# Gathering ready-made key and value rows in the attention edge stage of a graph kernel

## The chip, the cores and the metric

One Trainium2 chip, one of its cores. The metric is the device time of one execution in microseconds (us), the median over several runs; lower is better.

## The reference

Four message-passing layers run over one graph of 50,000 nodes and 50,000 edges, the edges sorted by destination `dst`, 128 features throughout. The change touches the second layer, a sparse attention with 8 heads of 16 features. Its input is `h`, the node features behind a layer norm and a ReLU:

```python
K = (h @ Wk.T + bk).reshape(N, 8, 16)
V = (h @ Wv.T + bv).reshape(N, 8, 16)
Q = h.reshape(N, 8, 16)
scores = sum(K[src] * Q[dst], -1) / 4
attn = softmax of scores over the edges of one dst, per head
out = segment_sum(V[src] * attn[:, :, None], dst)
h_attn = out.reshape(N, 128) @ Wo.T + bo
```

A batch norm, a feed-forward block and two more layers follow (a gated layer and one with a weight for each of 8 relations), and the kernel gives back the last node features.

## The kernel before

The rows, nodes or edges, are cut into 98 steps of 512 rows (`S = 98`, four tiles of 128, `TILES = 4`). Ten stages run one behind the other, with a barrier between them, and each runs its 98 steps as a software pipeline written out by hand: every engine has its own list of instructions, the loop counter `i` or `n` is the same on all, and an engine works in its turn `n` on step `n - lag`. The order within a turn is the order in the code, and semaphores tie the engines together. In the trace `n_` stands ahead of the tiles of node stages, `e_` ahead of those of edge stages.

**`mean_nodes`** (930 to 1497 us) ends the first layer and prepares the second. For each step SP (SyncE) loads 4 tiles of run sums (L981) and x (L987), DVE (VectorE) builds a 0/1 matrix `pick` (L1079), PE (TensorE) multiplies the two (L1014, `mean_done`), DVE computes x1 (L1027 to L1055) and its norm statistics, ACT (ScalarE) applies norm and ReLU in 4 instructions (L277, called from L1101), which gives `h1`. ACT also issues the stores of x1 (L1094) and h1 (L1105). POOL (GpSimd) scatters h1 with 4 indirect DMAs (L709, called from L998) into the table `at_first`, each node's row to the place of its first edge. `h1` has four buffers, and ACT writes one again only when its scatter has landed (`scattered`).

**`attention_edges`** (1506 to 2341 us) has three stretches.

- In turn `n` POOL gathers the `h1` rows of the source nodes, 512 B each, with 4 indirect DMAs (L701, called from L1250) into `hs` (4 buffers, free again after `hs_turned`). SP loads `hd` and `keep`. PE transposes `hs` (L1535), ACT copies the result to `hst` (L1457), which has `HELD = 30` buffers, because it is needed again 28 turns later. PE multiplies by `wk` (L1542) in turn n+2, DVE forms key times query, `kq` (L1402) in turn n+3, from the keys in PSUM and `hdt`, which a scan fills (L1410); PE adds up each head's score (L1527).
- Once in 14 steps (`GROUP`) the softmax of 14 steps is computed by ten short chains of DVE and PE, one in each turn, so that its weights `weight_t` exist some 30 turns after the gather.
- From turn 30 on PE multiplies `hst` by `wv` (L1564), DVE multiplies the values in PSUM by the weights, `pv` (L1420), and builds another 0/1 matrix, `pick` (L1443), and PE sums the edges of one node, `ps_p` (L1574). The sum of a run that crosses a border of 256 edges is carried: `carry_step` on DVE (L1388, L1390) waits for `pack_done`, adds the carry to the first column of each half of `ps_p` in PSUM and keeps the last column of each. Then ACT copies `ps_p` with a bias to `att` (L1486), PE multiplies by `wo` (L1556), ACT copies to `packed` (L1480, six buffers), and SP writes each half of it to `att_runs` (L1238). Before it writes a half, SP waits until the half before has landed (`placed`), because they overlap.

From SP's turn 98 there is nothing left to load, and SP also issues three stores of zeros in each turn (L1214) for a later stage, in 33 turns. Gathers, `hst`, `kq` and scores end with turn 98 to 101 as well; values, sums and output go on for 36 turns more. `ps_hs`, `ps_hd`, `ps_k`, `ps_v`, `ps_p`, `ps_r`, `ps_s`, `ps_x` take one PSUM bank each, all eight.

Of the kernel before, what the change touches and what calls it, by code (L numbers as in the profile page):

```python
# [7 lines left out]
ALU = mybir.AluOpType  # L8
# [8 lines left out]
P = 128  # L17
# [264 lines left out]
class Kept:  # L282


    def __init__(self, nc, ctx, size):
        def tile(name, shape, dt=F32):
            return ctx.enter_context(nc.sbuf_tensor(name, shape, dt))

        self.ident = tile("ident", [D, D])
        self.w1_node = tile("w1_node", [D, D])  # L290
        self.w1_edge = tile("w1_edge", [D, D])
        self.wk = tile("wk", [D, D])
        self.wv = tile("wv", [D, D])
# [60 lines left out]
def prepare(nc, size, a, scratch, out, k):  # L354

    S = size.steps
    with Phase(nc, "prep") as ph:
# [78 lines left out]
        def _(sp):  # L436
# [6 lines left out]
            for tile, src in (  # L443
                (w2, a["L0_W2"]),
                (k.wk, a["L1_WkT"]), (k.wv, a["L1_WvT"]), (k.wo, a["L1_WoT"]), (k.w_node, a["L2_W_node"]),
                (w_center_t, a["L2_W_centerT"]), (w_cat_node, a["L2_W_cat"][0:D, :]),
                (k.w_cat_sum, a["L2_W_cat"][D:2 * D, :]), (k.w_edge, a["L2_W_edge"]),
                (b1, a["L0_b1"]), (k.bk, a["L1_bk"]), (k.bv, a["L1_bv"]), (k.bo, a["L1_bo"]),
                (k.ff_b1, a["L1_b1"]), (k.ff_b2, a["L1_b2"]), (k.bn, a["L1_bn"]),
            ):  # L450
                sp.dma_start(tile[:, :], src[:, :]).then_inc(weights_in, 16)
# [496 lines left out]
def mean_nodes(nc, size, a, scratch, k):  # L948
# [5 lines left out]
    with Phase(nc, "n0") as ph:  # L954
# [11 lines left out]
        x1_out, h1_out = ph.dma_sems("x1_out"), ph.dma_sems("h1_out")  # L966
# [3 lines left out]
        ps_m = [[ph.ps(f"m{u}{b}", (P, HALVES, D + 1)) for b in range(HALVES)] for u in range(2)]  # L970
        block = ph.ctx.enter_context(nc.Block())
# [33 lines left out]
        def _(pe):  # L1005
# [11 lines left out]
            each_step(body, S, 1)  # L1017
# [70 lines left out]
        def _(act):  # L1088
            def body(i, u):
# [16 lines left out]
            each_step(body, S, 5)  # L1106
            for u in range(SLOTS):
                act.wait_ge(x1_out[u], all_moved(S, u))
                act.wait_ge(h1_out[u], all_moved(S, u))


def attention_edges(nc, size, a, scratch, k):
# [10 lines left out]
    with Phase(nc, "e1") as ph:  # L1123
        idx, idx_in = ph.sb("idx", [P, S, 2 * TILES], I32), ph.sem("idx_in")
        half, half_in = ph.sb("half", [P, S, 2 * HALVES]), ph.sem("half_in")
        hs, hs_in = ph.loaded("hs", [P, TILES, D])
# [5 lines left out]
        hst, hst_ready = ph.made("hst", [D, ROWS], HELD)  # L1132
# [4 lines left out]
        att, att_ready = ph.made("att", [D, ROWS])  # L1137
# [5 lines left out]
        hs_turned, hd_turned, k_done, score_done = (ph.sem(n) for n in ("hs_turned", "hd_turned", "k_done", "score_done"))  # L1143
        v_done, pack_done, out_done, carry_done = (ph.sem(n) for n in ("v_done", "pack_done", "out_done", "carry_done"))
# [31 lines left out]
        ps_hs, ps_hd, ps_k, ps_v, ps_p, ps_r = (ph.ps(n) for n in ("hs", "hd", "k", "v", "p", "r"))  # L1176
# [21 lines left out]
        def _(sp):  # L1198
# [4 lines left out]
            for n in range(STEPS + 6):  # L1203
# [27 lines left out]
                w = n - 40  # L1231
# [11 lines left out]
        @block.gpsimd  # L1243
        def _(pool):
            pool.wait_ge(idx_in, 16)
            for i in range(S):
                if i >= 4:
                    pool.wait_ge(hs_turned, i - 3)
                pool.sem_inc(pool_turn, 1)
                gather(pool, at(hs, i), scratch["h1"], idx[:, i, :], 0, at(hs_in, i))  # L1250

        @block.vector
        def _(dve):
# [141 lines left out]
            for n in range(STEPS):  # L1395
                j = n - 3
                if 0 <= j < S:
                    dve.wait_ge(k_done, j + 1)
# [3 lines left out]
                    dve.scalar_tensor_tensor(at(kq, j)[:, :], flat(ps_k), k.bk[:, :], at(hdt, j)[:, :], ALU.add, ALU.mult  # L1402
# [11 lines left out]
                if 0 <= j < S:  # L1414
                    g, t = divmod(j, GROUP)
                    dve.wait_ge(v_done, j + 1)
# [7 lines left out]
                if 0 <= n - 32 < S:  # L1424
                    carry_step(n - 32)
# [23 lines left out]
        def _(act):  # L1449
            act.wait_ge(consts_ready, 3)  # L1450
            for n in range(STEPS):
                j = n - 1
                if 0 <= j < S:
                    act.wait_ge(hs_turned, j + 1)
                    if j >= HELD:
                        act.wait_ge(v_done, j - HELD + 1)
                    act.activation(at(hst, j)[:, :], flat(ps_hs), ACT.Copy).then_inc(hst_ready, 1)  # L1457
# [17 lines left out]
                j = n - 34  # L1475
# [6 lines left out]
                if 0 <= j < S:  # L1482
                    act.wait_ge(carry_done, j + 1)
                    if j >= 2:
                        act.wait_ge(out_done, j - 1)
                    act.activation(at(att, j)[:, :], flat(ps_p), ACT.Identity, bias=k.bv[:, :]).then_inc(att_ready, 1)  # L1486
# [10 lines left out]
        def _(pe):  # L1497
# [22 lines left out]
            for n in range(STEPS):  # L1520
# [9 lines left out]
                if i < S:  # L1530
                    pe.wait_ge(at(hs_in, i), moved(i, i, TILES))
                    if i:
                        pe.wait_ge(hst_ready, i)
                    for t in range(TILES):
                        ins = pe.transpose(ps_hs[:, t, :], at(hs, i)[:, t, :], k.ident[:, :])  # L1535
                    ins.then_inc(hs_turned, 1)
                j = n - 2
                if 0 <= j < S:
                    pe.wait_ge(hst_ready, j + 1)
                    if j:  # L1540
                        pe.wait_ge(kq_ready, j)
                    pe.matmul(flat(ps_k), k.wk[:, :], at(hst, j)[:, :], start=True, stop=True).then_inc(k_done, 1)  # L1542
                if i < S:
# [6 lines left out]
                j = n - 33  # L1550
                if 0 <= j < S:
                    pe.wait_ge(att_ready, j + 1)
# [5 lines left out]
                j = n - 29  # L1558
                if 0 <= j < S:
                    pe.wait_ge(hst_ready, j + 1)  # L1560
                    if j:
                        pe.wait_ge(pv_ready, j)
                    for t in range(TILES):
                        ins = pe.matmul(ps_v[:, t, :], at(hst, j)[:, t * P:(t + 1) * P], k.wv[:, :], start=True, stop=True)  # L1564
                    ins.then_inc(v_done, 1)
                j = n - 31
                if 0 <= j < S:
                    pe.wait_ge(pv_ready, j + 1)
                    pe.wait_ge(pick_ready, j + 1)
                    if j:  # L1570
                        pe.wait_ge(att_ready, j)
                    for t in range(TILES):
                        h = t // HALVES
                        ins = pe.matmul(flat(ps_p)[:, h * HALF:(h + 1) * HALF], at(pv, j)[:, t, :], at(pick, j)[:, t, :],  # L1574
# [1076 lines left out]
```

## Time and profile before

| what | value |
|---|---|
| median of 3 runs | 5954.6 us (5951.74 to 5968.38) |
| profiled execution | 5969.23 us, of which 5967.4 us are the span from its first to its last instruction |
| mean granted TensorE clock | 0.809 of full speed |
| stage `mean_nodes` | 930 to 1497 us |
| stage `attention_edges` | 1506 to 2341 us |
| busy share of the span | PE 63%, DVE 66%, ACT 34%, POOL 51% |

The profile gives one execution. In its rows PE is TensorE's matmuls, PEld its weight loads, DVE, ACT and POOL the engines; SPq, ACTq and POOLq are the issues of DMAs by an engine's queue. A stage's speed is best told as us for one step. DMA share is the mean busy share of the 16 DMA engines; packets of one engine can overlap, so it can be over 1. Shares over the whole span mix ten stages with different limits, and only those of one stretch say what binds there.

### The profile page before, as it was taken

Reading aid. Unit: us, or ns where it says so; the run is one execution under the profiler, and the core shown is the slowest. Engines: PE = TensorE matmul, PEld = TensorE weight load, DVE = VectorE, ACT = ScalarE, POOL = GpSimd, SP = SyncE. Lnnn points to the kernel's source line nnn. Section 1 sums busy time; section 2 is a strip of 40 time slices with the busy share of each in tenths; the row PEclk is TensorE's granted clock in tenths of the full one; section 3 lists DMA queues with packets and bytes.
Section 4 is the critical chain, followed back from the end, with each engine's and each line's share of the span. In section 5 each row is a group of like instructions: output and inputs, shape, how many; then the busy total and the mean of one; then the engine's idle time right before and its main releaser. Section 6 shows DMA issues by size and latency. Waiting matters only on the chain. (4 is left out here: it accounts for less than half of the span.)

```text
span 5967.4 us, 85405 instructions
## 1 busy us (share of the span) xinstructions
PE 3748.6 (63%) x16668; PEld 2531.9 (42%) x16668; DVE 3959.9 (66%) x12622; ACT 2012.0 (34%) x4449; POOL 3039.3 (51%) x2764
## 2 busy tenths in 40 slices
PE   0788883333599985579965566666400199889830
PEld 0566662332367764544455545555300044334310
DVE  8555556887388863654455555656488788888856
ACT  0555542333122221235565632222144333333310
POOL 0655534777676600000077767777700367777730
PEclk9888885555799998999967778888855599999975
DMA  6677766776455545877677767777588511111149
GB/s 228 151 174 173 172 159 192 219 217 176 125 132 144 142 161 170 276 246 229 219 243 231 227 170 130 131 130 128 88 280 271 156 31 39 43 46 47 49 162 375
DMA packets 986574, 996.40 MB, mean 167 GB/s; under 512 B 210641, under 2 KB 648417, under 8 KB 986163
## 3 DMA queue, kind: packets, MB, share of 16 engines
q1 hardware_dynamic: 676899, 628.12, 37.1%
q0 software_dynamic: 131904, 146.31, 12.6%
q10 hardware_dynamic: 177488, 218.95, 10.3%
q8 instruction: 86, 1.41, 0.1%
q14 instruction: 197, 1.61, 0.1%
HBM read 560.95 MB, written 466.16 MB: 172 GB/s over the span
## 5 line engine op out<-in xcount | busy, mean ns | idle before, releaser
L709 POOL DMA_INDIRECT at_first_table<-n_h,n_first_edge x784 | 811.5, 1035 | 1247.3 <-ACT n_h L277 901.1
L2495 PE MATMUL e_m<-e_by_rel,rel_w 128*128 128x512 f32 x1568 | 718.3, 613 | 0.0
L701 POOL DMA_INDIRECT e_xs<-x_table,e_idx x392 | 377.6, 963 | 516.0 <-POOLq L2385 396.8
L701 POOL DMA_INDIRECT e_x<-x,e_idx x392 | 408.2, 1041 | 371.8 <-DMA e_idx<-idx_table 261.3
L701 POOL DMA_INDIRECT e_hs<-h_table,e_idx x392 | 423.3, 1080 | 170.3 <-issue 110.9
L2409 DVE SCALAR_TENSOR_TENSOR e_by_rel<-e_y,e_part_t 128x512 f32<-128x512 f32 x784 | 476.0, 678 | 31.4 <-PE e_y L2510 24.0
L709 POOL DMA_INDIRECT rel_sum_table<-e_res,e_again x392 | 392.6, 1001 | 148.6 <-issue 125.2
L2495 PEld LDWEIGHTS e_m<-e_by_rel,rel_w 128*128 128x128 f32 x1568 | 302.6, 198 | 346.6 <-issue 346.6
L277 ACT ACTIVATE n_h<-n_x,n_norm_shift,n_norm_rstd 128x128 f32<-128x128 f32 x784 | 321.8, 482 | 327.1 <-issue 266.2
L1014 PE MATMUL n_m<-n_mean,n_pick 128*128 128x129 f32 x784 | 204.7, 442 | 356.2 <-DVE n_pick L1079 352.7
L2487 PE MATMUL e_t<-ident,e_part 128*128 128x128 f32 x392 | 70.1, 307 | 561.0 <-ACT e_part L277 442.6
L253 ACT ACTIVATE e_norm_std<-e_norm_moments,eps 128x4 f32<-128x4 f32 x196 | 58.3, 298 | 977.6 <-DVE e_norm_moments L245 972.5
L717 POOL DMA_INDIRECT sum_table<-e_res,e_target x196 | 309.8, 1581 | 141.6 <-issue 57.2
L1014 PEld LDWEIGHTS n_m<-n_mean,n_pick 128*128 128x128 f32 x784 | 175.6, 329 | 385.3 <-DVE n_pick L1079 381.5
L717 POOL DMA_INDIRECT sum_high_table<-e_res,e_target x196 | 307.4, 1568 | 60.2 <-issue 58.5
L2487 PEld LDWEIGHTS e_t<-ident,e_part 128*128 128x128 f32 x392 | 46.0, 153 | 581.6 <-ACT e_part L277 442.8
L2204 PE MATMUL e_p<-w_node,e_hdt 128*128 128x128 f32 x784 | 137.2, 328 | 233.1 <-DVE e_hdt L2140 232.9
L238 DVE BATCH_NORM_STATS2 e_norm_stats<-e_x 128x6 f32<-128x128 f32 x392 | 85.4, 280 | 273.8 <-DMA e_x<-x,e_idx 273.8
L2204 PEld LDWEIGHTS e_p<-w_node,e_hdt 128*128 128x128 f32 x784 | 115.2, 226 | 272.5 <-DVE e_hdt L2140 223.5
L253 ACT ACTIVATE n_norm_std<-n_norm_moments,eps 128x4 f32<-128x4 f32 x294 | 86.1, 293 | 425.0 <-DVE n_norm_moments L245 379.7
L2168 DVE TENSOR_TENSOR e_target<-e_shift,dump_row 128x4 int32<-128x4 f32 x98 | 16.0, 163 | 288.4 <-DMA sum_high_table<-e_res,e_target 288.2
L2179 ACT ACTIVATE e_keep<-e_f 128x512 f32<-128x512 f32 x98 | 58.5, 597 | 433.0 <-PE e_f L2216 433.0
(373 smaller groups left out, 10428.9 us busy)
## 6 DMA issues: line engine op xcount, KB each, us to landing
x_table<-n_x ACTq DMA_DIRECT2D x294, 256.0 KB
n_x<-x_table SPq DMA_DIRECT2D x294, 256.0 KB
e_hd<-at_first_table SPq DMA_DIRECT2D x196, 256.0 KB
mean_runs_table<-e_packed SPq DMA_DIRECT2D x196, 130.0 KB
n_mean<-mean_runs_table SPq DMA_DIRECT2D x392, 65.0 KB
at_first_table<-prep_zero ACTq DMA_DIRECT2D x1, 25088.0 KB
e_edge<-edge128T SPq DMA_DIRECT2D x98, 256.0 KB
e_keep<-col_tab_table SPq DMA_DIRECT2D x196, 128.0 KB
```

Source lines behind the costliest of these rows:

```text
L238: last = dve.bn_stats(at(self.stats, u)[:, t, :], x[:, t, :])
L253: act.activation(at(self.std, u)[:, :], at(self.moments, u)[:, :, 1], ACT.Sqrt, bias=k.eps[:, :]).then_inc(self.std_done, 1)
L277: last = act.activation(out[:, t, :], x[:, t, :], func, bias=at(self.shift, u)[:, t:t + 1], scale=at(self.rstd, u)[:, t:t + 1])
L701: pool.indirect_dma_start(out=tile[:, t, :], out_offset=None, in_=table, in_offset=bass.IndirectOffsetOnAxis(ap=idx[:, col + t:col + t + 1 ...
L709: pool.indirect_dma_start(out=table, out_offset=bass.IndirectOffsetOnAxis(ap=idx[:, t:t + 1], axis=0), in_=tile[:, t, :], in_offset=None, ...
L717: pool.indirect_dma_start(out=table, out_offset=bass.IndirectOffsetOnAxis(ap=idx[:, t:t + 1], axis=0), in_=tile[:, t, :], in_offset=None, ...
L1014: ins = pe.matmul(at(ps_m, u - 1)[t // HALVES][:, t % HALVES, :], at(pick, u - 1)[:, t, :], at(mean, u - 1)[:, t, 0:D + 1], start=True, st ...
L2179: act.activation(at(keep, u)[:, :], flat(ps_f), ACT.Copy).then_inc(keep_ready, 1)
L2204: ins = pe.matmul(ps_p[:, t, :], at(hdt, u - 1)[:, t, :], k.w_node[:, :], start=True, stop=True)
L2409: ins = dve.scalar_tensor_tensor(at(by_rel, u - 5)[:, r, :], flat(ps_y), float(r), at(part_t, u - 5)[:, :], ALU.is_equal, ALU.mult)
L2487: ins = pe.transpose(ps_t[:, t, :], at(part, u - 3)[:, t, :], k.ident[:, :])
L2495: ins = pe.matmul(flat(at(ps_m, u - 6)), k.rel_w[:, r, :], at(by_rel, u - 6)[:, r, :], start=(r == 0), stop=(r == RELS - 1))
```

## The change

Keys and values are computed once for each node, in `mean_nodes`, and not for each edge. The node stage transposes `h1` on PE, copies it on ACT, multiplies by the joined weight `wkv` (128 x 256), copies the 128 x 1024 result on ACT, and ACT issues a third store of 512 KB in each step, into a new table `key_val` of 1 KB rows. The edge stage gathers these 1 KB rows. PE transposes only their key half, and DVE forms `kq` from that in turn n+2; the value half is copied by ACT from `hs` to `val` (30 buffers). The products with `wk` and `wv` are gone, and `pv` reads `val` in SBUF. The two free banks give `ps_hs` and `ps_p` two buffers each. ACT copies `ps_p` to `att` before the carry is added (and its last columns to `tails`); the carry is added in `att`, in SBUF, one turn later, and what follows moves by a turn.

```diff
# mean_nodes, TensorE (after the product with pick; loop now S + 8 turns)
+                j = i - 8
+                    pe.wait_ge(h1t_ready, j + 1)
+                    for t in range(TILES):
+                        ins = pe.matmul(ps_kv[t // HALVES][:, t % HALVES, :], at(h1t, u)[:, t, :], k.wkv[:, :], start=True,
+                                        stop=True)
+                    ins.then_inc(key_val_done, 1)
+                j = i - 6
+                    pe.wait_ge(h1_ready, j + 1)
+                    for t in range(TILES):
+                        ins = pe.transpose(ps_h[:, t, :], at(h1, u - 6)[:, t, :], k.ident[:, :])
+                    ins.then_inc(h1_turned, 1)
# mean_nodes, ScalarE (after the store of h1; loop now S + 10 turns)
+                        act.wait_ge(h1_turned, j - 3)      # before norm.apply writes h1
+                j = i - 7
+                    act.activation(at(h1t, u - 7)[:, :, :], ps_h[:, :, :], ACT.Copy).then_inc(h1t_ready, 1)
+                j = i - 9
+                    for b in range(HALVES):
+                        ins = act.activation(at(key_val, u - 9)[:, HALVES * b:HALVES * b + HALVES, :], ps_kv[b][:, :, :],
+                                             ACT.Copy)
+                j = i - 10
+                    act.dma_start(rows_of(scratch["key_val"], j), flat(at(key_val, u - 10))
+                                  ).then_inc(at(key_val_out, u - 10), 16)
# attention_edges
-        ps_hs, ps_hd, ps_k, ps_v, ps_p, ps_r = (ph.ps(n) for n in ("hs", "hd", "k", "v", "p", "r"))
+        ps_hs, ps_hd, ps_p, ps_r = ph.banks("kt"), ph.ps("qt"), ph.banks("p"), ph.ps("r")
-                w = n - 40
+                w = n - 41
# GpSimd
+                    pool.wait_ge(val_ready, i - 3)
-                gather(pool, at(hs, i), scratch["h1"], idx[:, i, :], 0, at(hs_in, i))
+                gather(pool, at(hs, i), scratch["key_val"], idx[:, i, :], 0, at(hs_in, i))
# VectorE
-                dve.wait_ge(pack_done, j + 1)
+                dve.wait_ge(att_ready, j + 1)
-                    own = flat(ps_p)[:, h * HALF:(h + 1) * HALF]
+                    begin = at(att, j)[:, h * HALF:h * HALF + 1]
-                                             own[:, HALF - 1:HALF], ALU.mult, ALU.add)
-                    done(dve.scalar_tensor_tensor(own[:, 0:1], held[0][:, :], half[:, j, h:h + 1], own[:, 0:1],
-                                                  ALU.mult, ALU.add))
+                                             at(tails, j)[:, h:h + 1], ALU.mult, ALU.add)
+                    done(dve.scalar_tensor_tensor(begin, held[0][:, :], half[:, j, h:h + 1], begin, ALU.mult, ALU.add))
-                                      ps_v[:, :, :].rearrange("p t (h c) -> p t h c", c=HEAD_DIM),
+                                      at(val, j)[:, :, :].rearrange("p t (h c) -> p t h c", c=HEAD_DIM),
# ScalarE
-                    act.activation(at(hst, j)[:, :], flat(ps_hs), ACT.Copy).then_inc(hst_ready, 1)
+                    act.activation(at(val, j)[:, :, :], at(hs, j)[:, :, D:2 * D], ACT.Copy).then_inc(val_ready, 1)
-                    act.wait_ge(carry_done, j + 1)
-                    act.activation(at(att, j)[:, :], flat(ps_p), ACT.Identity, bias=k.bv[:, :]).then_inc(att_ready, 1)
+                    act.wait_ge(pack_done, j + 1)
+                    act.activation(at(tails, j)[:, :], flat(at(ps_p, j))[:, HALF - 1::HALF], ACT.Copy)
+                    act.activation(at(att, j)[:, :], flat(at(ps_p, j)), ACT.Identity, bias=k.bv[:, :]).then_inc(att_ready, 1)
# TensorE: the products with wk (turn n - 2) and wv (turn n - 29) are taken out
-                    pe.matmul(flat(ps_k), k.wk[:, :], at(hst, j)[:, :], start=True, stop=True).then_inc(k_done, 1)
-                        ins = pe.matmul(ps_v[:, t, :], at(hst, j)[:, t * P:(t + 1) * P], k.wv[:, :], start=True, stop=True)
+                    if i >= 2:
+                        pe.wait_ge(kq_ready, i - 1)
```

## Rows read from the trace of the kernel before

**Rows 1.** Five stretches: us, busy us by engine (instructions), clock, DMA share, GB/s.

```profile
1100.00:1300.00 200.00, 75.72 (x291) 64.74 (x290) 170.36 (x762) 66.10 (x180) 155.78 (x146) 0.50 0.75 218
1540.00:1660.00 120.00, 87.43 (x314) 46.79 (x313) 65.13 (x81) 17.35 (x28) 91.36 (x95) 0.84 0.51 132
1700.00:2050.00 350.00, 345.42 (x2040) 262.69 (x2040) 309.91 (x794) 100.47 (x177) 248.91 (x220) 1.00 0.54 141
2400.00:2600.00 200.00, 117.86 (x835) 105.08 (x835) 130.61 (x210) 48.14 (x70) 0.00 (x0) 0.93 0.88 276
5800.00:5900.00 100.00, 0.00 (x0) 0.00 (x0) 65.03 (x98) 0.00 (x0) 0.00 (x0) 0.50 1.09 381
```

In Rows 1 the engines stand in the order PE, PEld, DVE, ACT, POOL.

**Rows 2.** Groups of instructions, 1700 to 2050: busy us, mean ns | idle before, releaser.

```profile
L701 POOL DMA_INDIRECT e_hs<-h_table,e_idx x220 | 249.9, 1136 | 101.4 <-issue 62.3 <-PE e_hs L1535 39.1
L1574 PE MATMUL e_p<-e_pick,e_pv 128*128 128x256 f32 x424 | 100.3, 379 | 0.0
L1564 PE MATMUL e_v<-wv,e_hst 128*128 128x128 f32 x424 | 56.0, 275 | 0.0
L1542 PE MATMUL e_k<-e_hst,wk 128*128 128x512 f32 x104 | 53.2, 594 | 0.0
L1420 DVE TENSOR_TENSOR e_pv<-e_v,e_weight_t 128x512 f32<-128x512 f32 x52 | 35.4, 680 | 25.1 <-PE e_p L1574 24.3
L1480 ACT ACTIVATE e_packed<-e_r 128x512 f32<-128x512 f32 x53 | 31.7, 598 | 37.1 <-PE e_r L1556 33.4 <-DMA att_runs_table<-e_packed 2.6 <-issue 1.1
L1390 DVE SCALAR_TENSOR_TENSOR e_p<-e_carry,e_half,e_p 128x1 f32<-128x1 f32 x104 | 22.4, 216 | 0.0
```

**Rows 3.** SP's waits, 1700 to 2050: us in total, times, longest.

```profile
SPq L1238 <- DMA att_runs_table<-e_packed: 94.3, 50, 4.0
SPq L1230 <- DVE e_pick L1446: 31.6, 10, 5.1
SPq L1211 <- DVE e_hdt L1410: 3.8, 6, 1.0
```

**Rows 4.** Groups over the edge stage: a one-column instruction that works in SBUF.

```profile
L1384 DVE TENSOR_TENSOR e_carry<-e_carry,e_factor_col 128x1 f32<-128x1 f32 x6 | 1.0, 160 | 0.2
```

**Rows 5.** Timeline of the node stage: a scatter alone, and one beside DVE.

```profile
1109.40 0.98 POOL L709 DMA_INDIRECT at_first_table<-n_h,n_first_edge  x1 [0.31 <-issue]
...
1110.61 0.68 DVE L1047 SCALAR_TENSOR_TENSOR n_leaky<-n_biased 128x512 f32<-128x512 f32 x1
1110.68 1.46 POOL L709 DMA_INDIRECT at_first_table<-n_h,n_first_edge  x1 [0.30 <-issue]
```

**Rows 6.** Groups of instructions in the node stage, 930 to 1500.

```profile
L709 POOL DMA_INDIRECT at_first_table<-n_h,n_first_edge x392 | 425.8, 1086 | 227.9 <-DVE n_first_edge L1065 118.4 <-issue 109.2 <-ACT n_h L277 0.3
L1014 PE MATMUL n_m<-n_mean,n_pick 128*128 128x129 f32 x784 | 204.7, 442 | 356.2 <-DVE n_pick L1079 352.7 <-issue 3.5
```

**Rows 7.** Timeline, the node stage's end: ACT's last store, POOL's last scatter.

```profile
1479.46 0.33 ACTq L1105 DMA_DIRECT2D h_table<-n_h  x1
...
1496.14 0.98 POOL L709 DMA_INDIRECT at_first_table<-n_h,n_first_edge  x1 [0.31 <-issue]
```

**Rows 8.** ACT's DMA queue, 1100 to 1300: packets, MB, share of 16 engines; its issues.

```profile
q10 hardware_dynamic: 10584, 19.26, 25.9%
...
h_table<-n_h ACTq DMA_DIRECT2D x36, 256.0 KB
```

**Rows 9.** Timeline: the sums of one step at half clock.

```profile
2298.44 3.58 PE L1574 MATMUL e_p<-e_pick,e_pv 128*128 128x256 f32 x8
```

**Rows 10.** POOL's DMA queue, 1700 to 2050.

```profile
q0 software_dynamic: 7027, 14.39, 17.8%
```

**Rows 11.** Timeline of one SP turn past turn 98: start us, us.

```profile
2229.28 2.38 SPq L1238 DMA_DIRECT2D att_runs_table<-e_packed  x2
...
2235.64 2.38 SPq L1238 DMA_DIRECT2D att_runs_table<-e_packed  x2
```

**Rows 12.** Waits of the next node stage, 2400 to 2600: us in total, times, longest.

```profile
PE n_h L1706 <- DMA n_h<-h_table: 82.0, 61, 4.0
```

More of the change, by code:

```diff
@@ L291, in __init__ @@
         self.w1_edge = tile("w1_edge", [D, D])
-        self.wk = tile("wk", [D, D])
-        self.wv = tile("wv", [D, D])
+        self.wkv = tile("wkv", [D, 2 * D])
         self.wo = tile("wo", [D, D])
@@ L965, in mean_nodes @@
         h1, h1_ready = ph.made("h1", [P, TILES, D], 4)
-        x1_out, h1_out = ph.dma_sems("x1_out"), ph.dma_sems("h1_out")
+        h1t, h1t_ready = ph.made("h1t", [D, TILES, P])
+        key_val, key_val_ready = ph.made("key_val", [P, TILES, 2 * D], 4)
+        x1_out, h1_out, key_val_out = ph.dma_sems("x1_out"), ph.dma_sems("h1_out"), ph.dma_sems("key_val_out")
+        h1_turned, key_val_done = ph.sem("h1_turned"), ph.sem("key_val_done")
         kept_ready, mean_done, copy_turn = ph.sem("kept_ready"), ph.sem("mean_done"), ph.sem("copy_turn")
@@ L970, in mean_nodes @@
         ps_m = [[ph.ps(f"m{u}{b}", (P, HALVES, D + 1)) for b in range(HALVES)] for u in range(2)]
+        ps_h = ph.ps("h")
+        ps_kv = [ph.ps(f"kv{b}", (P, HALVES, 2 * D)) for b in range(HALVES)]
         block = ph.ctx.enter_context(nc.Block())
@@ L1016, in body @@
                     ins.then_inc(mean_done, 1)
-            each_step(body, S, 1)
+                j = i - 8
+                if live(j, S):
+                    pe.wait_ge(h1t_ready, j + 1)
+                    if begun(j - 1):
+                        pe.wait_ge(key_val_ready, j)
+                    for t in range(TILES):
[3 more added lines that the diff above has]
+                j = i - 6
+                if live(j, S):
+                    pe.wait_ge(h1_ready, j + 1)
+                    if begun(j - 1):
+                        pe.wait_ge(h1t_ready, j)
+                    for t in range(TILES):
+                        ins = pe.transpose(ps_h[:, t, :], at(h1, u - 6)[:, t, :], k.ident[:, :])
+                    ins.then_inc(h1_turned, 1)
+            each_step(body, S, 8)
         @block.vector
@@ L1105, in body @@
                     act.dma_start(rows_of(scratch["h1"], j), flat(at(h1, u - 5))).then_inc(at(h1_out, u - 5), 16)
-            each_step(body, S, 5)
+                j = i - 7
+                if live(j, S):
+                    act.wait_ge(h1_turned, j + 1)
+                    if begun(j - 2):
+                        act.wait_ge(key_val_done, j - 1)
+                    act.activation(at(h1t, u - 7)[:, :, :], ps_h[:, :, :], ACT.Copy).then_inc(h1t_ready, 1)
+                j = i - 9
+                if live(j, S):
+                    act.wait_ge(key_val_done, j + 1)
+                    if begun(j - 4):
+                        act.wait_ge(at(key_val_out, u - 9), moved(j - 4, u - 9))
+                    for b in range(HALVES):
+                        ins = act.activation(at(key_val, u - 9)[:, HALVES * b:HALVES * b + HALVES, :], ps_kv[b][:, :, :],
+                                             ACT.Copy)
+                    ins.then_inc(key_val_ready, 1)
+                j = i - 10
+                if live(j, S):
+                    act.wait_ge(key_val_ready, j + 1)
+                    act.dma_start(rows_of(scratch["key_val"], j), flat(at(key_val, u - 10))
+                                  ).then_inc(at(key_val_out, u - 10), 16)
+            each_step(body, S, 10)
             for u in range(SLOTS):
+                act.wait_ge(key_val_out[u], all_moved(S, u))
                 act.wait_ge(x1_out[u], all_moved(S, u))
@@ L1125, in attention_edges @@
         half, half_in = ph.sb("half", [P, S, 2 * HALVES]), ph.sem("half_in")
-        hs, hs_in = ph.loaded("hs", [P, TILES, D])
+        hs, hs_in = ph.loaded("hs", [P, TILES, 2 * D])
         hd, hd_in = ph.loaded("hd", [P, TILES, D])
@@ L1131, in attention_edges @@
         group_keep_in, group_tail_in = ph.dma_sems("group_keep_in", 2), ph.dma_sems("group_tail_in", 2)
-        hst, hst_ready = ph.made("hst", [D, ROWS], HELD)
+        val, val_ready = ph.made("val", [P, TILES, D], HELD)
         hdt, hdt_ready = ph.made("hdt", [D, ROWS], 3)
@@ L1136, in attention_edges @@
         pick, pick_ready = ph.made("pick", [P, TILES, HALF])
-        att, att_ready = ph.made("att", [D, ROWS])
+        att, att_ready = ph.made("att", [D, ROWS], 4)
+        tails = ph.slots(4, "tails", [D, HALVES])
         packed, packed_ready = ph.made("packed", [P, TILES, D], 6)
@@ L1142, in attention_edges @@
         pool_turn = ph.sem("pool_turn")
-        hs_turned, hd_turned, k_done, score_done = (ph.sem(n) for n in ("hs_turned", "hd_turned", "k_done", "score_done"))
-        v_done, pack_done, out_done, carry_done = (ph.sem(n) for n in ("v_done", "pack_done", "out_done", "carry_done"))
+        hs_turned, hd_turned, score_done = (ph.sem(n) for n in ("hs_turned", "hd_turned", "score_done"))
+        pack_done, out_done, carry_done = (ph.sem(n) for n in ("pack_done", "out_done", "carry_done"))
         head_win, consts_ready = ph.sb("head_win", [D, 2 * GH - HEADS]), ph.sem("consts_ready")
@@ L1202, in _ @@
             sp.wait_ge(zero_ready, 1)
-            for n in range(STEPS + 6):
+            for n in range(STEPS + 7):
                 i = n
@@ L1395, in _ @@
             for n in range(STEPS):
-                j = n - 3
+                j = n - 2
                 if 0 <= j < S:
-                    dve.wait_ge(k_done, j + 1)
+                    dve.wait_ge(hs_turned, j + 1)
                     if j >= 2:
@@ L1415, in _ @@
                     g, t = divmod(j, GROUP)
-                    dve.wait_ge(v_done, j + 1)
+                    dve.wait_ge(val_ready, j + 1)
                     dve.wait_ge(weight_t_ready, g + 1)
@@ L1474, in _ @@
                                    ).then_inc(weight_t_ready, 1)
-                j = n - 34
+                j = n - 35
                 if 0 <= j < S:
@@ L1549, in _ @@
                     ins.then_inc(hd_turned, 1)
-                j = n - 33
+                j = n - 34
                 if 0 <= j < S:
-                    pe.wait_ge(att_ready, j + 1)
+                    pe.wait_ge(carry_done, j + 1)
                     if j:
@@ L1557, in _ @@
                     ins.then_inc(out_done, 1)
[L1558 to L1563, printed above, removed]
-                        ins = pe.matmul(ps_v[:, t, :], at(hst, j)[:, t * P:(t + 1) * P], k.wv[:, :], start=True, stop=True)
-                    ins.then_inc(v_done, 1)
                 j = n - 31
@@ L1569, in _ @@
                     pe.wait_ge(pick_ready, j + 1)
-                    if j:
-                        pe.wait_ge(att_ready, j)
+                    if j >= 2:
+                        pe.wait_ge(att_ready, j - 1)
                     for t in range(TILES):
                         h = t // HALVES
-                        ins = pe.matmul(flat(ps_p)[:, h * HALF:(h + 1) * HALF], at(pv, j)[:, t, :], at(pick, j)[:, t, :],
+                        ins = pe.matmul(flat(at(ps_p, j))[:, h * HALF:(h + 1) * HALF], at(pv, j)[:, t, :], at(pick, j)[:, t, :],
                                         start=(t % HALVES == 0), stop=(t % HALVES == HALVES - 1))
@@ L2643 @@
     scratch["rel_sum"] = table("rel_sum", (R, D))
+    scratch["key_val"] = table("key_val", (R, 2 * D))
     scratch["tt"] = table("tt", (D, R))
```

26 lines of the change are left out of this document (9 added, 17 removed).

## The prediction

> **What bounds the kernel now.** The stages run one behind the other, so the busy shares of the whole span say little. I read the busy time by stretch first, and in it the two stages that the change touches, then for each of them the groups of instructions, the waits, and the DMA queues.
>
> In the middle of the edge stage PE is busy 345.4 of 350 us at full clock, DVE 309.9, and POOL is at 248.9 [rows 1]. The 424 matmuls of L1574 are 8 for each step, so 53 steps ran in 350 us: 6.60 us for one [rows 2]. PE is the bound there. The reader is to see how near the others stand behind it, because the change takes work from PE alone:
>
> - DVE: its one large wait for PE is 25.1 us, ahead of `pv` [rows 2]. Without it 53 steps take 324.9 us: 6.13 us for one.
> - SP: its waits for DVE are 31.6 and 3.8 us [rows 3]. The rest is its own issues, the reading of addresses, and the waits for `placed`, 94.3 us or 1.8 us for each step, which stay. (350 - 35.4) / 53 = 5.94 us.
> - POOL: a gather is 249.9 us busy and 62.3 us between issues over 220 instructions [rows 2], 1.42 us each, 5.68 us for four.
>
> In the first 30 turns POOL is the bound, 91.4 us busy in 95 gathers of 120 us, which is 5.05 us for four, while PE is at 87.4 us [rows 1]. PE's work there can shrink without effect. Past turn 98 the pace is SP's: one turn takes from 2229.28 to 2235.64, 6.36 us [rows 11], full of its own issues, the three stores of zeros among them.
>
> In the node stage PE is busy 75.7 of 200 us at half clock, DVE 170.4, and POOL 155.8 with its gap between two scatters not counted [rows 1]. Busy and gap together, (425.8 + 109.2) / 392 = 1.365 us for a scatter, are 5.46 us for a step [rows 6], and 36 stores of h1 in 200 us say 5.55 us [rows 8]. POOL is the bound, and it runs behind the others: the last store of h1 is issued at 1479.46 and the last scatter begins at 1496.14 [rows 7]. DMA share is 0.75 there [rows 1], which is 4.16 us of all 16 engines in each step.
>
> **The change, edge stage, turns 30 to 98.** PE loses the products with `wk`, 53.2 / 53 = 1.00 us, and with `wv`, 56.0 / 53 = 1.06 us [rows 2]. That leaves 4.5 us, and PE is no longer the bound. What is late next is DVE, SP or POOL.
>
> DVE: `kq` moves up a turn and reads PSUM as before. `pv` now reads `val` in SBUF; its width is the same, and I take the 680 ns that it has. The two pairs of carry instructions move to SBUF: 216 ns each now [rows 2], 160 ns for the nearest one that works in SBUF [rows 4], so 4 x 0.056 = 0.2 us less. Their new wait, for `att_ready` of a step that ACT worked off a turn earlier, holds up the group chains and `pick` behind it, but should be met. 6.13 - 0.2 = 5.93 us. If nothing comes of the carry, 6.13.
>
> ACT: the copy to `val` takes the place of the one to `hst`, 0.6 us, and `tails` is a small one more, at most 0.2 us by the one-column row [rows 4]. ACT is busy 100.5 of 350 us [rows 1], so that is covered. If ACT came late, `att` would be, and with it the carry and PE's product with `wo`. ACT's wait for the carry goes; it was on no path that sets the end.
>
> POOL: the number of gathers stays, a row is 1 KB. No 1 KB gather stands in this trace. From below the issue costs what it does now, 1.42 us. The transfer costs at most twice: the queue's share, 17.8% of 350 us over 53 steps, is 1.18 us of all engines [rows 10], and with as much again the DMA share would be 0.54 x 6.60 + 1.18 = 4.7 us of a step, which is covered. POOL has a second wait now, `val_ready`, four steps back, and ACT makes `val` one turn behind the gather, so three turns remain. The price is elsewhere: a scatter beside L1047, whose inputs both lie in SBUF, took 1.46 us, 0.48 more than one alone [rows 5]. The mean scatter of the node stage is 1.086 us [rows 6], 0.106 over those 0.98, so all such meetings cost 0.42 us a step there, with two instructions of this kind, L1047 and L1055. `pv` becomes one of this kind, so half of that, 0.2 us, is what I take; nothing from below, its full 0.68 us from above. POOL comes to 5.9 us (5.68 to 6.36).
>
> The Trainium skill, "SBUF — State Buffer", section "Who interferes with whom", says that a DVE instruction with two SBUF inputs contends with a GpSimd instruction that reads SBUF, and infers that descriptor generation, which writes, isn't held up by it. By that inference POOL's share of `pv` would be 0 and its step 5.68 us; by the row it is 5.9. The trace speaks against the inference in the node stage, for this place no run of before shows it.
>
> So DVE, SP and POOL stand at 5.93, 5.94 and 5.9 us. With one clear bound, PE, the step was 6.60 us against 345.4 / 53 = 6.52 us of busy time, 1% over. With three that hand on to each other, and DVE with long chains in ten of 14 turns, I take 4% over: 6.15 us (5.93 if they fit perfectly, 6.45 if POOL has the full 0.68 us and some wait with it). The stretch has 69 turns: 69 x (6.60 - 6.15) = 31 us less (10 to 46).
>
> **The first 30 turns and the end.** At the front POOL sets the pace and its work is the same: 0 (up to 5 us more, if 1 KB rows take 0.15 us longer a step). PE has less to do there and could fall to the lower clock level, as it is at 0.84 between the two with 73% busy [rows 1]; its work would still fit. At the end SP's turn is not shortened by anything. `w = n - 41` adds one turn without stores of zeros: two issues with their wait, 2.38 us [rows 11], and the reading of addresses ahead of them; I take 4 us. PE's remaining work there, L1574 and L1556 (of L1564's shape, 1.06 us), is 3.0 us at full clock [rows 2] and at half still under 6.36.
>
> **The node stage.** ACT gets three copies of 598 ns [rows 2] and an issue, 1.8 us on top of 66.1 / 36 = 1.84 us busy [rows 1, 8]: 3.6 of 5.46 us, covered; if it were late, h1 and then POOL would be. PE gets 8 more matmuls of 256 columns, 100.3 / 53 = 1.9 us at full clock [rows 2] or 3.6 at half [rows 9], and 4 transposes, about half of L1014's 204.7 / 98 = 2.09 us at half clock [rows 6]. With L1014 that is 6.7 us at half clock and 3.5 at full. At half clock it would not fit into 5.46 us, but then PE would be busy without a gap, and in every stretch where it was nearly that, the granted clock was 0.84 or more [rows 1]. DVE waits for `mean_done` only a whole step after `pick`, so an occasional late product costs nothing. DMA: the new store has as many bytes as those of x1 and h1 together, which are 25.9% of 200 us in 36 steps [rows 8], 1.44 us of all engines. 4.16 + 1.44 = 5.60 us against POOL's 5.46. A share of 1.09 is reached in another stage with 381 GB/s [rows 1]; here 0.75 would become 1.02 at the same pace. At 1.00 the step is 5.60 us, 14 us over the stage, and DVE, ACT and the loads have 16.7 us of lead on POOL to lose [rows 7]. The five more turns of ACT at the end fall under the same lead. At 0.95 it is 5.89 us: 42 - 17 = 25 us. I take 5 us (0 to 71, the upper end below).
>
> **The sum.** -31 + 4 + 5 = -22 us on the profiled execution's 5969.2 us (its span is 5967.4) gives 5947. That execution was 14.6 us over the median of the runs, so the median should be 5933 us. Measurements of this kernel tell about 0.3%, 18 us, from no change, so this is only just outside.
>
> **The rivals.**
>
> *The floors are reached*, 5.93 us a step and nothing lost in the node stage: -46 + 4 = -42 us, 5912. For it speaks that most waits look back a whole turn, against it that three engines would have to fit without loss. 0.16.
>
> *POOL takes PE's place*, with `pv` holding up a gather for its full length and 1 KB rows adding a little: 6.45 us a step, -10 + 4 + 5 = -1 us, 5953. For it: row and instruction of the same kind in [rows 5], and DVE's `pick` already costs POOL some of the 0.2 us by which a gather here is longer than at the front (1.136 against 91.4 / 95 = 0.96 us) [rows 1, 2]. Against: the gathers wait 39.1 us for PE [rows 2], so there is room. 0.22.
>
> *DMA becomes the bound of the node stage, and the kernel slower.* In the next node stage the share is 0.88 at 276 GB/s while PE waits for a load, 82 of 200 us [rows 1, 12]. If 0.88 is what a mix of 512 B packets and stores can reach, the step becomes 5.60 / 0.88 = 6.36 us, 88 - 17 = 71 us, and the sum -31 + 4 + 71 = +44 us: 5999. It decides from where the stage loses more than 27 + 18 = 45 us, a step of 6.09 us, a share under 0.92. Against it speaks the 1.09 [rows 1], with packets of another mix. 0.14.
>
> *The clock stays at half in the node stage*: (6.7 - 5.46) x 98 - 17 = 105 us, 6060. Against it stand all stretches with a busy PE. 0.06.
>
> **How the numbers follow.** My forecast has 0.42, 5915 to 5950, two thirds of that faster by over 0.3%. With the floors that makes 0.44 for faster; no change has 0.14 of the forecast and the POOL rival, 0.35 in all; slower 0.21. The range of 8 in 10 leaves out the half clock, most of the DMA rival's upper half and the best floors: 5905 to 5988.
>
> **What would show it.** In the middle of the edge stage 5.9 to 6.3 us a step, PE about 75% busy, DVE 95% and with hardly a wait for PE, SP's waits for DVE smaller. A gather beside `pv` longer than 0.94 us would bear out POOL's term. The end should keep its 6.36 us a turn and begin about 30 us earlier; the front 5.05 us. In the node stage DMA share 0.95 or more, PE at a clock over 0.5, the scatters back to back and the last one within some 5 us of where it was. The prediction is wrong if the node stage grows by over 20 us, or the middle stays over 6.4 us a step.

## The result, and the profile after

The changed kernel takes 6036.5 us (median of 4 runs, 6033.75 to 6051.78) against 5954.4 us for the kernel before: a ratio of 1.0136, 95% interval 1.0118 to 1.0154. It is 82 us slower, where 22 us faster was forecast. The span grew from 5967.4 to 6050.0 us.

The busy time by stretch of the changed kernel, columns as in [rows 1]; the first line is the node stage, the other two the front and the middle of the edge stage:

```profile
1100.00:1300.00 200.00, 130.87 (x703) 112.55 (x704) 167.40 (x750) 119.31 (x289) 156.40 (x144) 0.92 0.95 310
1560.00:1680.00 120.00, 79.06 (x235) 38.85 (x234) 59.08 (x75) 16.02 (x25) 91.46 (x94) 0.61 0.63 172
1750.00:2150.00 400.00, 292.61 (x1508) 205.91 (x1508) 311.74 (x796) 109.23 (x228) 243.87 (x212) 0.94 0.59 159
```

The node stage is as forecast in this execution: DMA share 0.95, PE's clock at 0.92, and the last scatter is issued 4.0 us later than in [rows 7]:

```profile
1500.15 0.98 POOL L708 DMA_INDIRECT at_first_table<-n_h,n_first_edge  x1 [0.30 <-issue]
```

The middle of the edge stage is not. In [rows 1] PE was busy 99% of it; now neither PE (73%) nor DVE (78%) nor POOL is, and yet a step takes longer. 53 steps stand in 400 us where 350 had sufficed. Read from the timeline, the stage comes apart like this. `kq` is its instruction on DVE, at L1402 before and L1446 after; 28 steps lie between the first and the 29th, 69 between that and the last.

| | first `kq` | to the 29th | to the last | a middle step | to the next stage's first instruction |
|---|---|---|---|---|---|
| before | 1530.3 | 141.6 | 456.1 | 6.61 | 215.8 |
| changed | 1526.6 | 165.3 | 518.3 | 7.51 | 225.9 |

So 24 us were lost in the front, 62 in the middle and 10 in the end, less 4 at the first `kq`: 92 us, of which later stages, which nobody changed, gave 10 back in this execution. `kq` is a turn earlier in the order now, so ahead of the first one a turn is gone (from the first gather to it 11.7 us, 20.4 before), and behind the last one stands one turn more: part of the 10 us is only that shift.

Who waits for whom in the middle, 1750 to 2150 us (us in total, times, longest):

```profile
ACT e_val L1501 <- DVE e_pv L1464: 159.9, 47, 4.8
...
POOL e_hs L700 <- ACT e_val L1501: 85.5, 29, 8.5
...
DVE e_kq L1446 <- issue: 74.6, 53, 4.0
PE e_kt L1580 <- DVE e_kq L1446: 52.6, 53, 1.0
PE e_qt L1586 <- DVE e_hdt L1454: 26.8, 48, 0.6
```

PE waits for `kq` in each of the 53 turns, and DVE stands still ahead of `kq` in each of them too. The timeline of one turn shows why:

```profile
1905.15 1.89 PE L1604 MATMUL e_p<-e_pick,e_pv 128*128 128x256 f32 x8
...
1906.08 0.17 DVE L1490 COPY e_pick<-e_row 128x4 f32<-128x4 f32 x1
...
1906.88 1.02 PE L1572 MATMUL e_s<-e_kq,e_head_win 128*112 128x512 f32 x2
...
1908.00 0.75 DVE L1446 SCALAR_TENSOR_TENSOR e_kq<-e_kt,bk,e_hdt 128x512 f32<-128x512 f32 x1 [1.75 <-issue]
...
1908.90 0.63 PE L1580 MATMUL e_kt<-ident,e_hs 128*128 128x128 f32 x4 [0.99 <-DVE e_kq L1446]
```

The first two lines end one turn of PE and DVE, the others begin the next. DVE ends its turn at 1906.25 and waits until PE has ended its own, with the sums of L1604, and has made the scores of the next (L1572). Only then comes `kq`, and only behind `kq` PE's transposes. Each engine hands the turn to the other once, and what either is late by stops both. The code says it too: `kq` has two buffers, and `dve.wait_ge(score_done, j - 1)` lets step j in only when the scores of step j-2 are made. Before, `kq` of turn n was step n-3, and the scores of step n-5 were PE's first work of turn n-1, long done. Now it is step n-2, and the scores of n-4 are PE's first work of the same turn. The change leaves that line as it was and moves `kq` a turn ahead (`j = n - 3` became `j = n - 2`).

### The profile page after: what moved, and what is told of

The parts are those of the page before. It is cut to its first block and busy times, and to the rows that moved or that the text cites. A ratio compares the mean times of both kernels' runs of the same rounds, so it can differ in the third digit from the quotient of the medians.

```text
span 6050.0 us, 86570 instructions
## 1 busy us (share of the span) xinstructions
PE 3823.5 (63%) x16864; PEld 2569.6 (42%) x16864; DVE 3959.3 (65%) x12622; ACT 2171.6 (36%) x4841; POOL 3047.7 (50%) x2764
## 5 line engine op out<-in xcount | busy, mean ns | idle before, releaser
L700 POOL DMA_INDIRECT e_hs<-key_val_table,e_idx x392 | 425.1, 1085 | 247.3 <-issue 118.7
L253 ACT ACTIVATE e_norm_std<-e_norm_moments,eps 128x4 f32<-128x4 f32 x196 | 58.3, 298 | 988.1 <-DVE e_norm_moments L245 966.4
L1027 PE MATMUL n_kv<-wkv,n_h1t 128*128 128x256 f32 x784 | 226.2, 439 | 173.1 <-ACT n_key_val L1140 171.4
L2234 PE MATMUL e_p<-w_node,e_hdt 128*128 128x128 f32 x784 | 135.2, 325 | 233.8 <-DVE e_hdt L2170 233.5
L238 DVE BATCH_NORM_STATS2 e_norm_stats<-e_x 128x6 f32<-128x128 f32 x392 | 85.5, 281 | 282.8 <-DMA e_x<-x,e_idx 282.8
L1027 PEld LDWEIGHTS n_kv<-wkv,n_h1t 128*128 128x128 f32 x784 | 161.1, 216 | 212.0 <-issue 189.5
L1604 PE MATMUL e_p<-e_pick,e_pv 128*128 128x256 f32 x784 | 209.8, 416 | 0.0
```

The lines of the kernel that those rows point to most:

```text
L238: last = dve.bn_stats(at(self.stats, u)[:, t, :], x[:, t, :])
L253: act.activation(at(self.std, u)[:, :], at(self.moments, u)[:, :, 1], ACT.Sqrt, bias=k.eps[:, :]).then_inc(self.std_done, 1)
L700: pool.indirect_dma_start(out=tile[:, t, :], out_offset=None, in_=table, in_offset=bass.IndirectOffsetOnAxis(ap=idx[:, col + t:col + t + 1 ...
L1027: ins = pe.matmul(ps_kv[t // HALVES][:, t % HALVES, :], at(h1t, u)[:, t, :], k.wkv[:, :], start=True, stop=True)
L1604: ins = pe.matmul(flat(at(ps_p, j))[:, h * HALF:(h + 1) * HALF], at(pv, j)[:, t, :], at(pick, j)[:, t, :], start=(t % HALVES == 0), stop=( ...
L2234: ins = pe.matmul(ps_p[:, t, :], at(hdt, u - 1)[:, t, :], k.w_node[:, :], start=True, stop=True)
```

## The experiments

Three theories. **S**: this handshake through `score_done`. **V**: the wait of ACT's copy to `val` for a `pv` one turn back, through which POOL loses 85.5 us. **D**: the transfers, in the node stage or as 1 KB rows.

**A third buffer for `kq`** (kq_three):

```diff
-        kq, kq_ready = ph.made("kq", [D, ROWS])
+        kq, kq_ready = ph.made("kq", [D, ROWS], 3)
-                    if j >= 2:
-                        dve.wait_ge(score_done, j - 1)
+                    if j >= 3:
+                        dve.wait_ge(score_done, j - 2)
```

> Edit: a third kq buffer, so that kq of step j waits for the scores of step j-3, which TensorE made a turn earlier, and no longer for those of the same turn. Theory S (the two engines hand every turn to each other through score_done): a step of the middle falls from 7.55 us to 6.0-6.4 and the kernel from 6036 to 5940-5960 us. Theory V (the wait of the copy to val for pv, one turn back, holds ScalarE and GpSimd): under 20 us gained, 6015-6036. Theory D (1 KB gathers and the fuller DMA engines): no gain, 6036.

**One more `val` buffer** (held_31): `HELD = 31`.

> Edit: 31 val buffers in place of 30, so that the copy to val waits for a pv two turns back. Theory V: the 85 us in which gathers wait for the copy to val go, and the kernel falls by 50 us or more. Theory S: that wait is a follower of the slow turn; under 10 us gained, 6026-6040 us. Theory D: 6036.

**Both** (kq_three_held_31), with `hdt` at two buffers and a wait for `kq_ready` to make room.

> Both edits (hdt with two buffers for the room). Theory S: as with the third kq buffer alone, 5935-5960, at most 15 us below it. If S and V bind one behind the other: clearly below both, by 20 us or more. The floors of the prediction (DVE, SP, GpSimd at 5.9 us a step) would show as 5920-5935 us.

**The node stage alone** (node_stage_only): `mean_nodes` of the changed kernel, `attention_edges` of before.

> Edit: the changed node stage with the edge stage of before, which still gathers h1; the key_val table is written and not read. The prediction priced the node stage at 5 us: 5955-5965 us. If the node stage itself had cost what is missing: 6000 us or more.

| kernel | us | ratio to before, interval | front | a middle step | end |
|---|---|---|---|---|---|
| kq_three | 5981.9 | 1.0038 (1.0025 to 1.0052) | 145.8 | 6.74 | 235.1 |
| held_31 | 6039.1 | 1.0137 (1.0120 to 1.0153) | 164.2 | 7.43 | 226.1 |
| kq_three_held_31 | 5978.2 | 1.0030 (1.0015 to 1.0046) | 146.3 | 6.67 | 233.5 |
| node_stage_only | 5961.5 | 1.0007 (0.9997 to 1.0018) | 143.0 | 6.60 | 217.8 |

S holds: the third buffer alone takes 55 us away, with it 20 of the front's 24 us. V falls: with one more `val` buffer nothing is gained, and POOL waits 58.3 of 300 us for PE's transposes in place of ACT. The node stage costs 4 us by the ratio (up to 11 by the interval), 6 by the medians; D falls as far as it meant that stage. But kq_three missed its 5940 to 5960, and kq_three_held_31 its 5935 to 5960: the middle went to 6.7 us, not to 6.0 to 6.4, and the end grew. SP's waits with the third buffer, 1750 to 2050:

```profile
SPq L1282 <- DMA att_runs_table<-e_packed: 108.8, 43, 3.8
SPq L1274 <- DVE e_pick L1490: 4.9, 3, 2.9
```

and the longest of the other engines there:

```profile
ACT e_packed L1524 <- DMA att_runs_table<-e_packed: 180.8, 37, 6.4
```

SP hardly waits for an engine any more, in [rows 3] it did for 35 us. 108.8 us over some 45 steps is 2.4 us of waiting for `placed` in each, against 1.8 before. SP seems to have become the bound, and `packed` is full behind it. This theory, **SP**, has two parts: SP's turn sets the pace, and the second 512 B of a row make the landings longer.

**SP writes a step's second half after the next turn's loads** (the late half), on kq_three_held_31, on the changed kernel, and on the kernel before; `place` waits for `placed` and writes one half, and its definition and its last call are not shown:

```diff
+            behind_half = []
+                if behind_half:                    # after hd, keep and the zero stores of the turn
+                    place(*behind_half.pop())
...
-                    for h in range(HALVES):
-                        if w or h:
-                            sp.wait_ge(placed, (w * HALVES + h) * 16)
-                        sp.dma_start(...)
+                    place(w, 0, begins)
+                    behind_half.append((w, 1, begins))
```

> Edit on kq_three_held_31 (5978 us): SP no longer waits in place for the first half of a step's rows to land, but writes the second half after the loads of the next turn. Theory SP (with the third kq buffer the edge stage is paced by SP, whose turn holds a wait of 2.5 us for placed): the middle falls from 6.5 to 5.9-6.2 us a step, the end from 6.4 to 4.6-5.2 us a turn, and the kernel to 5870-5910 us. Theory R (SP only follows, DVE or the gathers pace the middle): only the end gains, 5920-5950. If neither: 5978.

> The same edit of SP on the changed kernel as it is (6036 us), kq with two buffers. Theory S says the middle is held by the handshake and stays at 7.5 us a step; the end loses its SP turn, -50 to -65 us: 5970-5990 us. If SP were what holds the middle: 5930 or less.

> The same edit of SP on the kernel before (5955 us). The middle is bound by TensorE at 6.6 us a step and stays; the end falls from 6.4 to 4.6-5.2 us a turn, -45 to -60 us: 5895-5910 us. If SP's turn is not the bound of the end: 5955.

**Narrow rows** (three_31_narrow): on kq_three_held_31, `gather` reads `h1` into `hs[:, :, 0:D]`, and `val` is copied from there; the keys and values themselves are left out.

> Edit on kq_three_held_31 (5978 us): 512 B rows of h1 are gathered in place of 1 KB rows of key_val and used as keys and as values; so the keys and values themselves are left out of the result. Theory B (the second 512 B make the landings of SP's writes longer, 2.4 us of wait a step against 1.8 before, and through SP the step): the wait returns to 1.8-1.9 us, the middle to 5.9-6.1 us and the kernel to 5935-5955 us. Theory C (the landing is long for another reason, such as the shorter step itself): within 8 us of 5978.

These four ran on a chip on which the kernel before took 6521 us, so only ratios and stretches count: 1.0035 (1.0018 to 1.0053), 1.0164 (1.0142 to 1.0186), 0.9941 (0.9921 to 0.9962) and 1.0104 (1.0084 to 1.0124). There the late half shortened the end, 191.7 us against 232.8 for the narrow one without it, but hardly the middle, 6.67 against 6.77 us. On the changed kernel as it is the middle stayed at 7.78 us, as S says, though the late half left SP waiting for DVE's `pick` again, for 80.9 of 300 us (1900 to 2200):

```profile
SPq L1285 <- DVE e_pick L1500: 80.9, 29, 7.4
```

Set against the kernel before, what had been expected was 0.986 to 0.992, 1.003 to 1.006, 0.990 to 0.992 and 0.997 to 1.000, so all four missed: the edit on the kernel before by 0.2%, the other three by some 1%. Those three hold the changed node stage, which cost some 65 us, 1%, on that chip (last section).

The set was run once more on a chip like the first, with kq_three_held_31 in place of the changed kernel.

> The kernel of kq_three_held_31 again, as the base of the next three on one chip (their first runs fell on a chip on which the kernel before took 6521 us). On a chip like the first: 5970-5985 us, SP without a wait for an engine in the middle, 6.4-6.5 us a step.

> SP writes the second half after the next turn's loads. Theory SP: the middle falls to 5.9-6.2 us a step, SP waits for VectorE there again, the end falls by 40 us (as it did on the other chip, 191.7 against 232.8 us from the last kq to the next stage), the kernel to 5870-5920 us. Theory R: only the end gains, 5930-5945.

> The same SP edit on the kernel before: only the end gains, 30-40 us: 5915-5925 us (ratio 0.994 on the other chip).

> 512 B rows of h1 in place of 1 KB rows of key_val, used as keys and values; keys and values themselves are left out. Theory B: SP's waits for placed return to 1.8-1.9 us a step, the middle to 6.0 us and the kernel to 5940-5955 us. Theory C: 5970-5985 us, as with 1 KB rows.

| kernel (kernel before: 5937.0) | us | ratio to before, interval | front | a middle step | end |
|---|---|---|---|---|---|
| three_31_again | 5958.7 | 1.0035 (1.0018 to 1.0051) | 145.1 | 6.64 | 234.9 |
| three_31_late_again | 5889.3 | 0.9927 (0.9904 to 0.9951) | 145.5 | 6.37 | 191.8 |
| before_late_again | 5908.4 | 0.9942 (0.9925 to 0.9958) | 144.1 | 6.60 | 185.7 |
| three_31_narrow_again | 5934.0 | 0.9999 (0.9986 to 1.0013) | 147.0 | 6.20 | 234.8 |

The base, three_31_again, has the ratio it had before, though its middle came to 6.64 us and not to 6.4 to 6.5. Both parts of SP hold in the times; the narrow rows and the edit on the kernel before came out some 6 us below what was expected of them, the late half within it. With SP's second write behind the next turn's loads the same kernel is 69 us faster, 43 of them in the end and 19 in the middle. But the middle came to 6.37 us, not to 5.9 to 6.2, and SP didn't go back to waiting for DVE there. It still waits twice in each turn for landings, 1.7 us a step in all, against 2.4:

```profile
SPq L1252 <- DMA att_runs_table<-e_packed: 50.4, 46, 2.4
SPq L1253 <- DMA att_runs_table<-e_packed: 29.7, 44, 1.5
```

A turn of SP in the end can be 4.99 us there (5.4 in the mean of the turns with zeros, against 6.5 without the edit), not the 6.36 of [rows 11]:

```profile
2150.94 0.40 SPq L1253 DMA_DIRECT2D att_runs_table<-e_packed  x1
2151.38 1.45 SPq L1267 DMA_DIRECT2D rel_sum_table<-e_zero  x3
2153.02 0.40 SPq L1253 DMA_DIRECT2D att_runs_table<-e_packed  x1
2153.46 0.51 SPq L1285 DMA_DIRECT2D e_row<-row_tab_table  x1
2155.93 0.40 SPq L1253 DMA_DIRECT2D att_runs_table<-e_packed  x1
```

With narrow rows and the old SP turn, the waits for `placed` are 82.3 us in 48.5 steps, 1.7 us each, against 108.8 in 45 with wide rows:

```profile
SPq L1282 <- DMA att_runs_table<-e_packed: 82.3, 47, 3.4
```

and the middle is 0.44 us a step faster, 30 us; 25 us in the median. That is the price of the 1 KB rows in this kernel. What binds then is POOL, and for most of the middle of three_31_late_again too. Its gathers in 300 us of the middle, first with the late half, then with narrow rows:

```profile
L700 POOL DMA_INDIRECT e_hs<-key_val_table,e_idx x197 | 239.9, 1218 | 60.9 <-issue 58.4 <-PE e_kt L1592 1.8 <-ACT e_val L1513 0.6
```

```profile
L700 POOL DMA_INDIRECT e_hs<-h_table,e_idx x194 | 242.3, 1249 | 59.2 <-issue 55.5 <-PE e_kt L1582 2.4 <-ACT e_val L1503 1.2
```

Busy and gap fill 298.3 and 297.8 of 300 us. Four gathers cost 6.1 to 6.2 us, so in these stretches the middle can go no lower while POOL's work is what it is. With narrow rows `kq` keeps that pace: from step 28 to step 93 (counted from 0) one comes every 6.15 us, 10 to 17 us behind the issue of its step's last gather. With the late half it does so up to step 73, every 6.15 us, and PE's weight loads wait for gathered rows (1750 to 1850):

```profile
PEld e_kt L1592 <- DMA e_hs<-key_val_table,e_idx: 14.7, 10, 2.4
```

From step 73 to 93 a step takes 6.73 us, and `kq` falls back from 11 to 28 us behind its gathers: POOL isn't the bound any more. What stands still there is ACT, ahead of `packed` (1950 to 2070), which points at SP's landings again; that is argued, not shown.

```profile
ACT e_packed L1536 <- DMA att_runs_table<-e_packed: 70.5, 18, 6.1
```

three_31_late_again is the fastest kernel of this study, 0.9927 of the one before. The SP edit alone has 0.9942, and the two intervals overlap, so it isn't shown that the change with its repairs adds anything to it.

## Why the prediction was wrong

**The step that failed** is the one on `kq` in the working for DVE: "`kq` moves up a turn and reads PSUM as before". A moved step brings its waits along, and the wait for `score_done` was priced at nothing. It held up `kq` and all of DVE's turn behind it, and PE, which now waits for `kq` ahead of its transposes, was held in turn: 0.9 us a step more than before in the middle, where 0.45 less was forecast, and 24 us in the front, for which 0 was forecast. The third buffer shows it: 55 of the 82 us go with it. No rival had it; all of them looked at engines and queues as capacities, and this loss is a loop between two engines that were each some 75% busy.

**PE's clock in the front.** The prediction let it fall, as PE's work "would still fit". From 1600 to 1680 us it was 0.50, where the kernel before had 0.74 to 0.91, and PE's scores, now inside the loop, took 2.05 us instead of 1.02, with DVE waiting for them:

```profile
1628.56 2.05 PE L1572 MATMUL e_s<-e_kq,e_head_win 128*112 128x512 f32 x2
...
1630.70 0.75 DVE L1446 SCALAR_TENSOR_TENSOR e_kq<-e_kt,bk,e_hdt 128x512 f32<-128x512 f32 x1 [2.65 <-PE e_s L1572]
```

Over the whole front the clock was 0.62, with the third buffer 0.71. How the 20 us divide between the wait and the clock isn't shown. In the middle it was 0.94, and with the third buffer 0.95, so what the buffer gave back there isn't the clock's.

**The three floors**, taken 4% over as 6.15 us, stood at 6.4 (late half) to 6.7 us (without). SP's 5.94 assumed that the waits for `placed`, 1.8 us a step, "stay". They rose to 2.4 as the rows gathered doubled in bytes; the working had priced the wider rows against the capacity of the DMA engines and not as latency for another queue. The narrow rows show this for 25 us. POOL's 5.9 came out as 6.1 to 6.2.

**POOL and `pv`.** In the changed kernel's middle the 50 gathers that ran beside `pv` took 0.12 us longer than 0.94 on average; with the third buffer the 63 that met `pv` and not `pick` (1750 to 2050) took 0.06 longer, and before the 75 beside it took 0.94. So the contention exists, at about half of the 0.2 us a step that was taken (0.06 to 0.12 us for one or two of the four gathers). The working had laid the node stage's 0.42 us a step on two instructions; in the trace 0.30 fall on scatters that met L1047 or L1055 and 0.11 on those that met that stage's own `pick` (L1079), whose two inputs lie in SBUF as well. Half of 0.30 would have been nearer. The Trainium skill's inference in "SBUF — State Buffer" ("Who interferes with whom"), that descriptor generation escapes such an instruction, is nearer to the edge stage's 0.06 to 0.12 us than to the node stage's 1.46 us [rows 5], but both stages show an effect. What costs POOL most is `pick`, a `tensor_scalar`: 0.5 to 0.6 us for a gather that meets it, in every version. The same section of the Trainium skill names `tensor_scalar` among the instructions that can hold the port shared with GpSimd when their operands allow it, and the longer gathers agree.

**The carry.** Its instructions in SBUF take what they took in PSUM; the 0.2 us were not there:

```profile
L1433 DVE SCALAR_TENSOR_TENSOR e_carry<-e_carry,e_half,e_tails 128x1 f32<-128x1 f32 x106 | 22.9, 216 | 2.0
L1435 DVE SCALAR_TENSOR_TENSOR e_att<-e_carry,e_half,e_att 128x1 f32<-128x1 f32 x105 | 22.4, 214 | 0.0
```

The row taken for it, L1384, was of another instruction, `tensor_tensor` against `scalar_tensor_tensor` [rows 4].

**The node stage** came out right in this execution, 4 us against 5: PE's clock rose from 0.50 to 0.92 with the added work, and at a DMA share of 0.95 the scatters still set the pace. But from its first product to the edge stage's first gather the eight profiled executions of kernels with it on the chips at 5937 to 5955 us took 572 to 591 us, 583 in the mean, against 575 and 569 in the two without: 11 us more rather than 4. The longest (587 to 591) had a DMA share of 0.91 or 0.92 between 1100 and 1300 us, the shortest 0.95, so the DMA rival occurred in a small way, and the hit on 4 us has some luck in it. The half clock didn't occur. Its sum is wrong too: 105 us without the -27 of the edge stage that the other rivals carry. With them it would have been 6033 us, next to the measured 6036.5 by chance.

**The end** was SP's, as said. The added turn cost what was forecast: from SP's last store of zeros to its last write 36.9 us, against 32.6. The 10 us of the table are not to be set against the 4 of the forecast, as `kq`'s own shift is in them. With the third buffer it was 19, and the trace shows why: SP comes to its first store of zeros only 14.6 us ahead of the last `kq`, 26.0 before and 30.9 in the changed kernel, so it enters the end 11 us further behind.

**Left open**: what holds the last third of the middle of three_31_late_again at 6.7 us, and the price of the carry's move by itself, which was not tried.

## What to carry to other kernels

When a step moves to an earlier turn, go through every wait that it passes, the ones for its own output buffers too, and ask in which turn of the other engine each is met: one that moves into the same turn ties the engines together, and a buffer more was the cure here. Capacities of engines don't show such a loop; waits that occur once in every turn on both sides do. And when the bound is taken away, the next one's floor holds only if the latencies in it do: here more bytes on one queue lengthened the landings for which another queue stood waiting.

## What was not expected of the hardware

The DMA engines carried the node stage at a share of 0.95 and 310 GB/s with a mix of 512 B packets and large stores, and the scatters took 547.2 us from first to last, against 544.0 before. On the slower chip this was not so. From the stage's first product to the edge stage's first gather the three kernels with the changed node stage took 718 to 721 us there, and the one without (the node stage of before and the SP edit) 653 us, so the change of the stage cost 65 to 67 us, at a share of 0.75 to 0.81. In 100 us of three_31_late_half:

```profile
1050.00:1150.00 100.00, 56.19 (x314) 48.39 (x312) 69.17 (x316) 51.92 (x123) 66.33 (x58) 0.88 0.80 267
```

A change that only just fits on one chip is thus not neutral on all. The kernel before itself differed by 9.5% between chips (6521 against 5954 us), so kernels of different chips are compared here by their ratio to the kernel before on the same chip.
